# One block for the mixer: resolvent, join and Hebbian loop of a decoder kernel merged, row norms taken per tile, rows scaled by GpSimd

## The reference

```
h   = norm(x)                                  # 2048 rows of 256
V, u = (norm(h) * g1 + b1) @ w_pot + b_pot      # 2 numbers per row
gamma = softplus(u) + 0.1
G   = diagonal of inverse of tridiag(V + 2 - i*gamma, -1)   # two continued fractions over 1024 rows
h  += [Re G, Im G] @ w_bk + b_bk
q, k, v = (norm(h) * g2 + b2) @ w_qkv + b_qkv   # 8 heads of 64
W_t = exp(-gamma_t*0.01) * W_(t-1) + 0.1 * k_t v_t^T ;  o_t = q_t W_t
h  += o @ w_out + b_out
h  += gelu((norm(h) * g3 + b3) @ w_ff1 + b_ff1) @ w_ff2 + b_ff2
x   = x + h
```

## Time and profile before

| | us |
|---|---|
| median of 3 runs | 2088.84 (2085.67 to 2091.33) |
| profiled execution, its own time | 2089.83 |
| its span (first to last instruction) | 2087.8 |
| mean granted TensorE clock | 0.87 of full speed |
| TensorE busy | 1537.9 (74%) |
| VectorE busy | 1119.0 (54%) |
| ScalarE busy | 922.5 (44%) |
| GpSimd busy | 902.4 (43%) |

### The profile page before, as it was taken

One profiled execution on the slowest core, in us unless ns is written; L12 is line 12 of the kernel. 1 busy time (PEld: TensorE's weight loads), 2 busy tenths in 40 slices (PEclk: granted clock), 3 DMA queues, 4 the chain that ended last, 5 costly groups with the idle time before them and its releaser, 6 DMA issues. The chain is left out here.

```text
span 2087.8 us, 28529 instructions
## 1 busy us (share of the span) xinstructions
PE 1537.9 (74%) x9844; PEld 1286.0 (62%) x9844; DVE 1119.0 (54%) x2199; ACT 922.5 (44%) x1608; POOL 902.4 (43%) x722
## 2 busy tenths in 40 slices
PE   4787878889689638721269995977790499989990
PEld 1555665677468638710159994965780388878880
DVE  6667868788679512255664447447745123222322
ACT  4696986989344415321062227534241123222220
POOL 0598796998523345530042116030004205594406
PEclk8899999999899869955569996999895699999995
DMA  3001101010300325210000001020026102242103
GB/s 115 21 22 41 42 21 41 24 59 22 89 6 1 122 95 192 73 38 1 30 19 1 2 1 43 1 82 0 1 83 237 59 26 91 86 147 87 31 19 121
DMA packets 51960, 114.46 MB, mean 55 GB/s; under 512 B 13996, under 2 KB 34377, under 8 KB 44276
## 3 DMA queue, kind: packets, MB, share of 16 engines
q1 hardware_dynamic: 45060, 84.67, 11.7%
q0 software_dynamic: 6768, 28.02, 4.1%
HBM read 87.02 MB, written 25.87 MB: 54 GB/s over the span
## 5 line engine op out<-in xcount | busy, mean ns | idle before, releaser
L842 POOL TENSOR_TENSOR HC<-H,CB 128x512 f32<-128x512 f32 x256 | 321.7, 1278 | 109.5 <-DVE H L742 93.6
L573 ACT ACTIVATE UT<-DTXT,BT 128x512 f32<-128x512 f32 x256 | 181.3, 710 | 30.2 <-PE ps L419 29.8
L742 DVE TENSOR_TENSOR_SCAN H<-dA,ps 128x512 f32<-128x512 f32 x128 | 152.7, 1213 | 78.2 <-PE ps L419 67.2
L419 PE MATMUL ps<-ident,UT 128*128 128x128 f32 x1024 | 164.4, 285 | 40.5 <-ACT UT L573 21.0
L419 PEld LDWEIGHTS ps<-ident,UT 128*128 128x128 f32 x1024 | 122.0, 145 | 108.6 <-DVE H L742 38.5
L583 ACT ACTIVATE dA<-DT,nA 128x512 f32<-128x512 f32 x256 | 181.4, 710 | 11.4 <-DVE H L742 8.6
L428 PE MATMUL ps<-ident,HC 128*128 128x128 f32 x1024 | 156.9, 281 | 32.3 <-POOL HC L842 30.4
L742 DVE TENSOR_TENSOR_SCAN H<-dA,HL,ps 128x512 f32<-128x512 f32 x128 | 158.3, 1270 | 36.6 <-PE ps L419 29.9
L428 PEld LDWEIGHTS ps<-ident,HC 128*128 128x128 f32 x1024 | 120.4, 144 | 43.0 <-POOL HC L842 42.4
L1990 DVE TENSOR_TENSOR f_XN<-f_XN,ps 128x1024 f32<-128x1024 f32 x39 | 47.6, 1221 | 174.1 <-PE ps L147 174.1
L1766 POOL TENSOR_TENSOR f_W<-f_stage,f_zeros 128x2048 fp32r<-128x2048 f32 x18 | 64.9, 3605 | 167.0 <-POOLq L1783 166.7
(11 more groups left out here) (492 smaller groups left out, 4306.9 us busy)
## 6 DMA issues: line engine op xcount, KB each, us to landing
CB<-m_c_rows SPq DMA_DIRECT2D x16, 1024.0 KB, 4.6
f_w<-in_f_w SPq DMA_DIRECT2D x16, 1024.0 KB
f_stage<-in_f_w POOLq DMA_DIRECT2D x15, 1024.0 KB, 5.5
f_stage<-in_f_w SPq DMA_DIRECT2D x9, 1024.0 KB
f_rows_in<-f_zeros SPq DMA_DIRECT2D x13, 384.0 KB, 12.5
f_DI<-f_rows_in SPq DMA_DIRECT2D x39, 128.0 KB, 2.3
f_rows_out<-f_EO SPq DMA_DIRECT2D x39, 128.0 KB, 1.7
a_values<-a_zeros SPq DMA_DIRECT2D x8, 320.0 KB, 5.4
```

Source lines behind the costliest of these rows:

```text
L419: ins = pe.transpose(PS[4 + G % UR][:, t * P:(t + 1) * P], UT[:, n % 2, t, c * P:(c + 1) * P], g.ident[:, :])
L573: act.activation(UT[:, N % 2, t, :], DTXT[:, k % 2, t, :], ACT.Copy, scale=BT[:, k % 2, t, n:n + 1]).then_inc(ut_ready, 1)
L742: dve.tensor_tensor_scan(H[:, G % HR, :], dA[:, G % AR, :], PS[4 + G % UR][:, :], first, ALU.mult, ALU.add).then_inc(h_ready, 1)
L842: pool.tensor_tensor(HC[:, y, :], H[:, s, :], CB[:, n // 4 % CR, n % 4, :], ALU.mult).then_inc(hc_ready, 1)
```

## The change

`resolvent` and `hebbian` become one block, `mixer_core`; its third part, `gelu_ffn`, stays a block of its own without norm and weight loads. In detail:

- The first norm's statistics also give the second norm's variance (var1), so that h_XN is made from X directly and Hrow's own statistics are not taken. The gains g1, g2, g3 are multiplied into w_pot, w_qkv and w_ff1 (by GpSimd and ScalarE), and the biases b1, b2, b3 go through those weights in matmuls of one column into b_pot, b_qk, b_v and bf1.
- All weights of the three parts are loaded at the start.
- Both softplus calls are one.
- Decay tables and weight halves are made while the resolvent chain runs.
- Row correction, row norm, transposes and halves are one loop over tiles, with the first group of queries and keys in it. GpSimd scales the rows (`XR`).
- In the Hebbian loop the padded values VP and the masked products KVm are gone: `read_out` uses 64-column weights that write to either half of the partitions, and WS is updated block by block. The third norm, its transposes and halves are made per tile, and the halves of w_ff1 and w_ff2 are made by ScalarE and GpSimd in the last three tiles.

The core of the diff:

```diff
+            @block.sync
+            def _(s):
+                load_all(s, names, a, loaded)
+                load_all(s, w.first(), a, w_loaded)
+                load_all(s, w.second(), a, late_loaded)
                 s.wait_ge(pot_copied, 4)
...
+            @block.gpsimd
...
+                for t in range(NT):
+                    pool.wait_ge(rstd2_ready, t + 1)
+                    if t >= 2:
+                        pool.wait_ge(row_turned, t - 1)
+                    pool.tensor_scalar(XR[:, t % 2, :], Hrow[:, t, :], mv2[:, t, 0:1], rstd2[:, t:t + 1],
+                                       ALU.subtract, ALU.mult).then_inc(row_ready, 1)
...
+            @block.tensor
+            def _(pe):
+                pe.wait_ge(loaded, ALL)
+                for kd in range(KD):
+                    ins = pe.matmul(PS[7][0:2, 0:1], w_pot[:, kd, :], b1[:, kd:kd + 1], start=(kd == 0), stop=(kd == KD - 1))
+                ins.then_inc(bp_ready, 1)
...
+                potential(3)
+                pe.wait_ge(w_loaded, W_ALL)
+                for f in range(2 * PAIRS):
+                    for kd in range(KD):
+                        pe.matmul(PS[1][:, f:f + 1], w.w_qkv[:, kd, f * P:(f + 1) * P], w.b2[:, kd:kd + 1],
+                                  start=(kd == 0), stop=(kd == KD - 1))
...
+                pe.wait_ge(late_loaded, U_ALL)
+                for f in range(FC):
+                    for kd in range(KD):
+                        ins = pe.matmul(PS[3][:, 64 + f:65 + f], w.w1[:, kd, f * P:(f + 1) * P], w.b3[:, kd:kd + 1],
+                                        start=(kd == 0), stop=(kd == KD - 1))
+                ins.then_inc(ub_ready, 1)
...
+                for i in range(NT + 3):
+                    if i < NT:
+                        forward(i)
+                    if i >= 3:
+                        turn_row(i - 3)
+                    if i == 7:
+                        pe.wait_ge(low_ready, GT)
+                        pe.wait_ge(wl_ready, 3)
+                        pe.wait_ge(wb_added, 2)
+                    if 7 <= i < 15:
+                        query_key(0, i - 7)
...
                     for q in range(NP):
-                        out = PS[6][:, q * P:(q + 1) * P]
                         for h in range(2):
-                            pe.matmul(out, VP[:, r, 2 * q + h, :], PTm[:, r, h * NP + q, :], start=(h == 0), stop=False)
-                        ins = pe.matmul(out, WS[:, q, :], QS[:, r, q, :], start=False, stop=True)
+                            pe.matmul(PS[6][h * HDW:(h + 1) * HDW, q * P:(q + 1) * P], VV[:, r, q * P + h * HDW:q * P + (h + 1) * HDW],
+                                      PTm[:, r, h * NP + q, :], start=True, stop=False)
+                        ins = pe.matmul(PS[6][:, q * P:(q + 1) * P], WS[:, q, :], QS[:, r, q, :], start=False, stop=True)
...
+                for t in range(NT + 3):
...
+                    if t >= 3:
+                        turn(t - 3)
...
+            @block.vector
...
+                dve.wait_ge(ub_ready, 1)
+                dve.tensor_tensor(w.bf1[:, :], w.bf1[:, :], PS[3][:, 64:64 + FC], ALU.add).then_inc(ub_added, 1)
+                dve.wait_ge(sp_out, 1)
...
+                for i in range(NT + 4):
+                    if i < NT:
+                        correct(i)
+                    if 1 <= i <= NT:
+                        invert(i - 1)
+                    if i < NT:
+                        spread(i)
+                    if i >= 4:
+                        row_low(i - 4)
...
+                        for h in range(2):
+                            e = slice(h * HDW, (h + 1) * HDW)
+                            dve.scalar_tensor_tensor(WS[e, :, e], WS[e, :, e], dec[e, t:t + 1], kv[e, :, e],
+                                                     ALU.mult, ALU.add).then_inc(ws_ready, 1)
...
+                for t in range(NT + 3):
+                    if t < NT:
+                        values(t)
+                    if 2 <= t < NT + 2:
+                        add_out(t - 2)
+                    if t < NT:
+                        masked(t)
+                    if 2 <= t < NT + 2:
+                        normalize(t - 2)
+                    if t >= 3:
+                        keep_low(t - 3)
                     if 1 <= t <= NT:
                         update(t - 1)
```

More of the change, by code:

```diff
@@ L2072, in resolvent @@
+        names = [(w_pot[:, :, :], "h_w_pot"), (b1[:, :], "h_b1"), (g1[:, :], "h_g1"), (b_pot[:, :], "h_b_pot"), (w_bk[:, :], "h_w_bk")]
+        ALL, W_ALL, U_ALL = 16 * len(names), 16 * len(w.first()), 16 * len(w.second())
+        GT = 4
         with nc.Block() as block:
@@ L2101, in _ @@
                 pool.memset(GR[:, :], 1.0).then_inc(ones_ready, 1)
-                pool.memset(Q[:, :, :, :, :], 0.0).then_inc(ones_ready, 1)
+                pool.memset(WS[:, :, :], 0.0).then_inc(ws_clear, 1)
+                pool.tensor_scalar(mask[:, :], g.upper[:, :], ETA, None, ALU.mult).then_inc(pool_chain, 1)
+                pool.wait_ge(loaded, ALL)
+                pool.wait_ge(bp_ready, 1)
+                for k in range(KD):
+                    pool.tensor_scalar(w_pot[:, k, :], w_pot[:, k, :], g1[:, k:k + 1], None, ALU.mult).then_inc(pot_scaled, 1)
@@ new lines, in _ @@
+                pe.wait_ge(gamma_ready, 1)
+                pe.matmul(PS[3][:, 0:NT], g.upper[:, :], gamma[:, :], start=True, stop=True)
+                pe.matmul(PS[3][:, NT:2 * NT], g.ones[:, :], gamma[:, :], start=True, stop=True).then_inc(lc_ready, 1)
+                for j in range(4):
+                    for c in range(4):
+                        t = 4 * j + c
+                        ins = pe.matmul(PS[4 + j][:, c * P:(c + 1) * P], gamma[:, t:t + 1].to_broadcast([P, P]), g.upper[:, :],
+                                        start=True, stop=True)
+                    ins.then_inc(lb_ready, 1)
@@ new lines, in scores @@
+                def scores(t):
+                    r, tt = (t // GT) % 2, t % GT
+                    pe.wait_ge(qk_used, 8 * (t // GT + 1))
+                    if t >= 1:
+                        pe.wait_ge(pt_ready, t)
+                    else:
+                        pe.wait_ge(f_used, NT)
+                    for h in range(2 * NP):
+                        q, lo_ = h // 2, HDW * (h % 2)
+                        ins = pe.matmul(PS[4 + h % 2][:, q * P:(q + 1) * P], QK[lo_:lo_ + HDW, r, NP + q, tt * P:(tt + 1) * P],
+                                        QK[lo_:lo_ + HDW, r, q, tt * P:(tt + 1) * P], start=True, stop=True)
+                    ins.then_inc(s_ready, 1)
@@ new lines, in _ @@
+                dve.wait_ge(std1_ready, 1)
+                ch(dve.reciprocal(rstd1[:, :], std1[:, :]))
+                ch(dve.tensor_tensor(rstd1[:, :], rstd1[:, :], rstd0[:, :], ALU.mult))
+                for t in range(NT):
+                    dve.tensor_scalar(XN[:, t, :], g.X[:, t, :], mv0[:, t, 0:1], rstd1[:, t:t + 1],
+                                      ALU.subtract, ALU.mult).then_inc(xn_ready, 1)
+                    if t == 3:
+                        dve.wait_ge(bp_ready, 1)
+                        dve.tensor_tensor(b_pot[:, :], b_pot[:, :], PS[7][0:2, 0:1], ALU.add).then_inc(bp_added, 1)
```

850 lines of the change are left out of this document (467 added, 383 removed).

## The result

The changed kernel takes **2055.97 us** (median of 4 runs, 2055.61 to 2056.95) against 2087.26 of the kernel before beside it: ratio **0.9845, 95% interval 0.9828 to 0.9862**. The forecast was 2026.8 with a range of 2008 to 2044. The direction was right, the size was not: 31 us were gained of the 63 forecast. The profiled execution took 2056.12 us (span 2054.4).

What follows compares the result with a forecast made beforehand. TensorE bounds the Hebbian loop and GELU part, a VectorE chain the resolvent, serial steps three joins. From 2089.8: -11.5 - 0.4 - 34.2 + 5.3 - 28.7 + 6.5 = -63.0, giving 2026.8 us, range 2008 to 2044.

Steps and rivals of the forecast that it cites:

- Part 1: Head before the first scan step: norm passes removed, transposes and potentials interleaved; scan at 945.2, 11.5 us earlier.
- Plus 0.3 and the 2.6 us of softplus: Head's last term: from the end of TensorE's bias products at 942.3 to the scan at 945.2.
- Part 2: Resolvent: second softplus goes but lay beside Q's transfer; 0.4 us saved, GpSimd's new work there taken as 0.
- Part 3: Last resolvent step to first values: one loop of 19 rounds, 37.0 us instead of 71.2, 34.2 saved.
- Part 4: Hebbian loop, bound by TensorE: added transposes 3.1 us, 64-column matmuls 2.2, together +5.3.
- rival (a): Hebbian loop: 64-column matmuls don't overlap and each excursion is paid, +15.6 instead of +2.2 us, 2040; chance 0.20.
- (b): Hebbian loop: 64-column matmuls overlap and edges are cheap, -13.4 instead of +2.2 us, 2011; chance 0.14.
- 0.245 for one excursion: Hebbian loop: price in us of one change from full-width into half-width matmuls and back, four per tile.
- Parts 5 and 6: Loop to GELU: one tile's chain, 4.5 us left, 28.7 saved; GELU part: TensorE stops behind GpSimd's additions, +6.5.
- Rival (c): Join before the first values: GpSimd's row scaling stretches VectorE's rounds through a shared memory port, +13, 2040; chance 0.12.
- Rival (d): Hebbian loop: half-width matmuls drop the clock to half, all 164.6 us doubled, 2191, slower than before; chance 0.03.

Runs made afterwards that it cites:

- e6: Against the changed kernel, GpSimd's large weight and mask work moved to VectorE's waits, w1's scaling to the Hebbian loop's first two tiles; 2039.47 us, ratio 0.9758.
- e4: Against the changed kernel, GpSimd adds the last bias to X in the Hebbian loop instead of at the GELU part's start; 2047.17 us, ratio 0.9800.
- e8: The changed kernel with the edits of both e6 and e7; 2034.56 us, ratio 0.9727.
- e3: Against the changed kernel, ScalarE instead of GpSimd scales the rows between resolvent and Hebbian loop; 2059.61 us, ratio 0.9859.
- e7: Against the changed kernel, only the order changed: potentials turned and softplus taken before the bias products and additions; 2056.32 us, ratio 0.9834.
- e9: Against the changed kernel, a hundred 128x512 products added on idle TensorE ahead of the join before the first values; 2057.03 us, ratio 0.9850.

## Why the prediction was wrong, step by step

In one sentence: the prediction gave VectorE's small instructions in head and scan their undisturbed durations and put GpSimd's new work beside them at 0, and that work held them for some 17 us.

**Part 1 (head, off by 13.2) failed.** TensorE was at the end 1.4 us late, bias products done at 943.7 instead of 942.3, but by errors that offset each other: the head's first steps came sooner (transposes at 914.9 instead of 916.3, b2's products at 929.3 instead of 930.5), b2's 32 records took 4.8 us for 3.6 and the four wide ones 3.7 for 1.7, at granted clocks of 0.73 and 0.50, and b3's took 4.6 for 5.4. (The row of 8.62 us for 16 records, too, is four at 0.85 and twelve at 0.43, not half and half.) What failed is "Plus 0.3 and the 2.6 us of softplus": I took the softplus at its undisturbed duration and never asked what GpSimd, whose weight scaling and low halves the change puts into the same 20 us, does to VectorE. I looked for what the change *waits* for, and this is no wait. The held scaling alone has 11.05 of the 13.2. e6 removes GpSimd's work and lands on 945.16 for the forecast 945.2; that it agrees to 0.04 is luck, for the reasons just given.

**Part 2 (resolvent, off by 5.4)** is the same cause: "GpSimd now works in this stretch, so between 0 and 1 us might be given back; I take 0." It gave back 5.9 in L2637 alone (12.9 instead of 7.0); the term was mis-sized by six times its own bound. e6 brings the stretch to 61.7.

**Part 3 (join, off by 3.9)** was right in form. First add after 3.9 (4.1), seven rounds 10.2 (10.5), round 7 5.1 (3.9), the next seven 16.7 (14.6), drain 5.0 (3.9). Mis-sized: forward matmuls and transposes that take turns cost TensorE 1.77 us a round at half clock, where I had added 0.87 and 0.43 (measured are 1.15 and 0.62, and 0.62 is what the earlier trace rows have for two transposes, 10.00 us in 16 tiles), and 0.82 at full clock, where I had 0.68; six products took 1.56 for 1.40. So a round with products at full clock is 2.38, not 2.08, and TensorE, not VectorE, sets the early rounds. Where the clock rises is worth 4 us more in e4, 6 in e8 and 7 in e3: a range that I had put at 2 us.

**Part 4 (loop, off by 7.4)** was right in kind: narrow matmuls overlap at 0.056 each, so rival (a) at its 3.64 a tile is out, and (b), cheap edges, is out too: 3.06. The mis-sized term is "0.245 for one excursion", which is 0.34; with the turn at 0.31 instead of 0.22 the tile is 8.76, not 8.43, or 5.3 us in 16 tiles. The other 2 lie at the loop's start, where the clock was at half after the drain (0.50 in 1065 to 1070).

**Parts 5 and 6** held: 4.9 for 4.5, and a stop of TensorE where it was forecast, with 7.2 for 6.5.

**Rival (c), the shared port,** was the right mechanism at the wrong place. I had its row before me (0.94 in the earlier trace rows for the 0.42 of the earlier trace rows) and priced it for the join's loop, where the operands are in PSUM or single, and where indeed nothing was held (the row add takes 0.39 to 0.42 beside GpSimd's scaling); I didn't carry it to the head and the scan, whose instructions are all in SBUF. Rival (d), the clock of the whole loop, was out: 0.99. The range failed for the same reason: none of its cases had the hold. Without it (e6, 2039.5) the time would lie inside.

## What to carry to other kernels

When work is put on an "idle" GpSimd, list the VectorE instructions that will run in the same microseconds. If they read two SBUF operands, or scale or copy from SBUF to SBUF, and lie on the path, one GpSimd instruction of 2 to 5 us stops a chain of 0.2 us links; put the large work where VectorE waits for a transfer (e6 did so with VectorE doing it; leaving it on GpSimd there was not run). Price a change of matmul width by a run of several excursions, not by one; and don't let TensorE stop briefly to save tenths.

## What the runs showed of the hardware that I had not expected

- Beside GpSimd's two-operand instructions VectorE's SBUF forms are held to their end (2.0 us of 2.35, and one instruction across three of them in a row, 9.40 us in e7; the 11.23 us are three and the last 1.9 us of a scaling). Beside a 128x1024 scaling the hold is only 0.7 to 0.8 of 2.77. Beside a 128x1536 scaling of 4.17 it is 2.9 to 3.0 for an instruction begun with it (3.18 and 3.07 us in e7), but one begun 1.3 us into it was held to its end (939.26 to 942.17 in the changed kernel).
- The clock fell in e9 after 3.65 us in which TensorE was busy for 2.40, and stayed at half while TensorE was 82 to 87% busy with 3-row matmuls and transposes (1030 to 1040). It rises at different moments in runs with almost the same work up to there (1043.9, about 1052, about 1056).
- GpSimd's scaling of 128x256 takes 1.22 us, longer than its addition of two tensors of that size (0.83).
